# Graph network kernel: more of the gathered rows fetched by SyncE, at byte offsets loaded into registers

## The chip, the cores and the metric

The kernel runs on 1 core of one Trainium2 chip. The metric is the device time of one execution in microseconds. A chunk below is 8 steps, and a step is one edge of each of the 128 partitions.

## The reference

Three message-passing rounds over the same graph of 6250 nodes and 100000 edges, sorted by destination, with rows of 256 float32. Cut to what matters:

```python
def conv(x):                                   # round 0
    e = relu((x[dst] - x[src]) @ theta_w.T + theta_b + x[src] @ phi_w.T + phi_b)
    return where(isfinite(m := segment_max(e, dst)), m, 0.0)
def layers(x, he):                             # rounds 1 and 2
    hv = x @ W_in + b_in
    for W, b in ((W_u0, b_u0), (W_u1, b_u1)):
        m = relu(concatenate([hv[src], he]) @ W + b)
        hv = where(has_in, segment_max(m, dst) + hv, hv)
    return relu(hv @ W_ro + b_ro)
x = layernorm(x + conv(x)); x = layernorm(x + layers(x, edge_attr))
```

## The kernel before

The products with the weights are taken per node, not per edge. Each round r first writes a table in HBM (`table{r}`, 6272 rows of 256 float32, 1 KB each), then walks the edges in 782 steps. Partition p holds 782 consecutive edges of the sorted list, and step t handles edge t of every partition. So a step needs 128 rows of the table, chosen by `src`.

**GpSimd** fetches them, one indirect DMA per step, into the ring `gath` of G = 34 steps (`gather_edges`, L606). A pair of steps is handed over by one semaphore, and a slot is free again when PE has summed the group that read it (`group_summed`). In round 0 the first 34 steps read `x` itself and go through transposes and a product (`multiply_raw`).

**PE** moves each pair of rows into a bank of `edge_ps` by a product with the identity (L864 in round 0, L887 in rounds 1 and 2, where the product with the edge attributes at L885 comes first). It may be up to 3 (round 0) or 6 pairs ahead of DVE.

**DVE** keeps the running maximum along the edges, one `SCALAR_TENSOR_TENSOR` per step (L410), in the ring `hist` of H = 24 steps, three chunks. Before it writes the first state of a chunk it waits until the store of the chunk that had the same place has landed (`stored`). In round 0 it also searches, once per 16 steps, for the last edge of each node (L338, L341).

**SyncE** stores each chunk of states to `runs` in HBM (`store_runs`, L547), all of its work in one queue and one order. Ahead of the store of chunk c it calls `late_rows(r, c)`, and in round 0, for 49 of the chunks from chunk 20 on, it loads a piece of `x` (L542). The last three chunks are stored in pieces of two steps.

`late_rows` is what the change rewrites. For two groups of LATE = 4 steps in each round, beginning at steps 360 and 720, GpSimd issues nothing and SyncE fetches the rows one at a time, 4 x 128 = 512 for a group, in 32 batches of 16, one batch ahead of each of 32 chunks (chunks 11 to 42 and 56 to 87). A batch is a load of 16 row numbers from HBM into 16 registers (L526, `TENSOR_LOAD`), and then for each row a register operation (L529, `snap` and the product of row number and row length) and a DMA of 1 KB whose source offset is in a register (L530). The row numbers lie in `late_src`, which two DMAs at the start copy out of `src` (L562). The rows land in `late_sb`, and PE waits for the whole group at its first step (`wait_rows`).

After the steps of a round, partitions' ends are joined (L615, L618), the maxima of the nodes are gathered (L633), and the tables for the next round are made. The change does not touch that.

Of the kernel before, what the change touches and what calls it, by code (L numbers as in the profile page):

```python
# [5 lines left out]
P = 128  # L6
NODES, EDGES, D, ED = 6250, 100000, 256, 64
# [3 lines left out]
STEPS = 2 * -(-EDGES // (2 * P))  # L11
STRIDE = TURNS * BODY
# [5 lines left out]
SC = 8  # L18
# [9 lines left out]
NPAD = TILES * P  # L28

NU = -(-TILES // 2)  # L30
ROUNDS = 3
# [7 lines left out]
LATE_AT = (360, 720)  # L39
LATE = 4  # L40
LATE_ROWS = 16
# [3 lines left out]
FIRST_X_CHUNK = 20  # L45
assert TURNS == TILES and STRIDE % SC == 0 and H % SC == 0 and G % GS == 0 and STRIDE % HC == 0 and HC % GS == 0 and SC % GS == 0
# [3 lines left out]
def gnn_kernel(nc, a):  # L50
    f32, bf16, i32 = mybir.dt.float32, mybir.dt.bfloat16, mybir.dt.int32
# [8 lines left out]
    late_src = nc.dram_tensor("late_src", [len(LATE_AT), P * LATE], i32, kind="Internal").ap()  # L60
# [4 lines left out]
    with ctx:  # L65
        def sb(name, shape, dt=f32):
            return ctx.enter_context(nc.sbuf_tensor(name, shape, dt))

        def sem(name):
            return ctx.enter_context(nc.semaphore(name))  # L70
# [13 lines left out]
        late_sb = sb("late_sb", [P, LATE, D])  # L84
# [104 lines left out]
        late_landed = [sem(f"late_landed{n}") for n in range(ROUNDS * len(LATE_AT))]  # L189
# [30 lines left out]
        def groups_to(s):  # L220
            return s // STRIDE * GROUPS + min(s % STRIDE // GS + 1, GROUPS)

        def late_group(t):
            return next((n for n, first in enumerate(LATE_AT) if first <= t < first + LATE), None)

        def by_pool(t):
            return t < STEPS and late_group(t) is None
# [4 lines left out]
        def edge_rows(s):  # L232
            n = late_group(s % STRIDE)
            if n is not None:
                return late_sb[:, s % STRIDE - LATE_AT[n]:s % STRIDE - LATE_AT[n] + 2, :]
            return gath[:, s % G:s % G + 2, :]
# [5 lines left out]
        def all_written(sems, n):  # L242
            return [(sems[b], 16 * uses(n, b)) for b in range(UNIT_BUFS)]
# [19 lines left out]
        setup_at = {}  # L263
# [22 lines left out]
        def _(dve):  # L286
# [21 lines left out]
            dve.wait_ge(edges_loaded, 16 * len(edge_loads))  # L308
            dve.wait_ge(bits_loaded, 16 * len(edge_bits))
# [183 lines left out]
        def _(sp):  # L493
# [6 lines left out]
            def write_table(r, u):  # L500
                lo, hi = unit(u)
                sp.wait_ge(product_out, r * NU + u + 1)
                sp.dma_start(tables[r][lo * P:hi * P, :].rearrange("(k p) f -> p k f", p=P),
                             staged(u)).then_inc(staged_written[u % UNIT_BUFS], 16)
# [5 lines left out]

            late_regs = [nc.sync.alloc_register(f"late_reg{k}") for k in range(LATE_ROWS)]

            def late_rows(r, c):
                for n, first in enumerate(LATE_AT):
                    batches = P * LATE // LATE_ROWS
                    i = c - (first // SC - 2 - batches)
                    if not 0 <= i < batches:
                        continue
                    if i == 0 and n == 0:
                        sp.wait_ge(late_listed, 16 * len(LATE_AT))  # L520
                        for written, m in all_written(staged_written, r + 1):
                            sp.wait_ge(written, m)
                    if i == 0 and r + n > 0:
                        before = (r, n - 1) if n > 0 else (r - 1, len(LATE_AT) - 1)
                        sp.wait_ge(group_summed, groups_to(before[0] * STRIDE + LATE_AT[before[1]] + LATE - 1))
                    nc.sync.load(late_regs, late_src[n:n + 1, i * LATE_ROWS:(i + 1) * LATE_ROWS])  # L526
                    for k, reg in enumerate(late_regs):
                        p, t = divmod(i * LATE_ROWS + k, LATE)
                        row = nc.sync.snap(reg, min_val=0, max_val=NPAD - 1)  # L529
                        sp.dma_start(late_sb[p:p + 1, t, :], tables[r][bass.DynSlice(row, 1), :]  # L530
                                     ).then_inc(late_landed[r * len(LATE_AT) + n], 16)
# [28 lines left out]
            for n, first in enumerate(LATE_AT):  # L560
                with nc.allow_non_contiguous_dma("small layouts"):
                    sp.dma_start(late_src[n:n + 1, :].rearrange("o (p k) -> (o p) k", k=LATE), a["src"][:, first:first + LATE]  # L562
                                 ).then_inc(late_listed, 16)
            for u in range(NU):
                write_table(0, u)
            sp.wait_ge(setup_step, setup_at["none row"])
# [205 lines left out]
        def _(pe):  # L772
# [70 lines left out]
            def wait_rows(s):  # L843
                r, t = divmod(s, STRIDE)
                n = late_group(t)
                if n is None:
                    pe.wait_ge(gathered[s % G // 2], 2 * 16 * pairs_in_slot(s))
                elif t == LATE_AT[n]:
                    pe.wait_ge(late_landed[r * len(LATE_AT) + n], 16 * P * LATE)
# [128 lines left out]
```

## Time and profile before

| | |
|---|---|
| median of 3 runs | 4386.74 us (4368.79 to 4420.99) |
| span of the profiled execution | 3216.1 us |
| median less span | 1170.6 us |
| GpSimd busy | 2359.0 us, 73% |
| PE busy | 2494.2 us, 78% |
| DVE busy | 1457.3 us, 45% |
| DMA engines, mean busy | some 70%, 237 GB/s |

The profiled execution is recorded by its span alone, from the first to the last instruction; the time that the runs report holds 1170.6 us more. The three edge phases, from the first store of `runs` to the last state of a round, are where the time goes: about 925, 954 and 957 us. DMA issues, register loads and register operations of SyncE are not counted as busy, so its own load is read from the times at which its instructions start (marked SPq).

### The profile page before, as it was taken

Reading aid. Unit: us, or ns where it says so; the run is one execution under the profiler, and the core shown is the slowest. Engines: PE = TensorE matmul, PEld = TensorE weight load, DVE = VectorE, ACT = ScalarE, POOL = GpSimd, SP = SyncE. Lnnn points to the kernel's source line nnn. Section 1 sums busy time; section 2 is a strip of 40 time slices with the busy share of each in tenths; the row PEclk is TensorE's granted clock in tenths of the full one; section 3 lists DMA queues with packets and bytes.
Section 4 is the critical chain, followed back from the end, with each engine's and each line's share of the span. In section 5 each row is a group of like instructions: output and inputs, shape, how many; then the busy total and the mean of one; then the engine's idle time right before and its main releaser. Section 6 shows DMA issues by size and latency. Waiting matters only on the chain.

```text
span 3216.1 us, 33579 instructions
## 1 busy us (share of the span) xinstructions
PE 2494.2 (78%) x6386; PEld 1183.3 (37%) x6386; DVE 1457.3 (45%) x3424; ACT 196.1 (6%) x439; POOL 2359.0 (73%) x2484
## 2 busy tenths in 40 slices
PE   8776666666676888887887888688888888888877
PEld 6432222222223533333333333353333344333335
DVE  2675556555556533333433334323333343333337
ACT  2000000000002400000000000010000000000005
POOL 5777777777776677777777777667777777777765
PEclk9898888788877999999999999899999999999989
DMA  7666667666665777777777777687777777777764
GB/s 263 232 223 222 225 224 268 221 224 214 211 210 191 246 242 244 245 244 244 245 252 246 245 244 247 207 271 249 250 251 252 252 267 247 253 249 252 250 210 153
DMA packets 266593, 762.66 MB, mean 237 GB/s; under 512 B 57652, under 2 KB 113823, under 8 KB 229903
## 3 DMA queue, kind: packets, MB, share of 16 engines
q0 software_dynamic: 118896, 324.63, 33.2%
q1 hardware_dynamic: 94110, 356.95, 28.8%
q10 hardware_dynamic: 53376, 78.93, 7.9%
q14 instruction: 158, 1.29, 0.1%
q8 instruction: 53, 0.87, 0.1%
HBM read 413.88 MB, written 346.41 MB: 236 GB/s over the span
## 4 chain that ended last, share of the span: by engine, by line
POOL 39%; PE 17%; DMA 16%; issue 16%; SPq 7%; DVE 2%; ACT 2%; DVEq 0%; ACTq 0%; POOLq 0%
POOL gath L606 38%; DMA gath<-table,src_sb 14%; PE edge_ps L887 6%; SPq L530 4%; PE edge_ps L885 3%; PE edge_ps L778 3%; SPq L526 2%; PE side_ps L778 2%; PE edge_ps L864 2%; POOL gath L633 1%; DVE hist L410 1%; ACT x_sb L718 1%; DMA runs<-hist 1%; SPq L529 1%; DMA table<-hist 1%
## 5 line engine op out<-in xcount | busy, mean ns | idle before, releaser
L606 POOL DMA_INDIRECT gath<-table,src_sb x2288 | 2165.4, 946 | 745.0 <-issue 649.6
L410 DVE SCALAR_TENSOR_TENSOR hist<-hist,lift,edge_ps 128x256 f32<-128x256 f32 x2346 | 1127.0, 480 | 1564.3 <-PE edge_ps L887 1142.8
L887 PE MATMUL edge_ps<-gath,ident 128*128 128x512 f32 x1548 | 842.6, 627 | 328.0 <-DMA gath<-table,src_sb 326.4
L885 PE MATMUL edge_ps<-w_e,he_sb 128*128 128x512 f32 x1564 | 813.9, 602 | 5.5 <-DMA he_sb<-in_he 5.0
L864 PE MATMUL edge_ps<-gath,ident 128*128 128x512 f32 x740 | 476.3, 767 | 269.9 <-DMA gath<-table,src_sb 164.2
L887 PEld LDWEIGHTS edge_ps<-gath,ident 128*128 128x128 f32 x1548 | 275.7, 193 | 803.9 <-DMA gath<-table,src_sb 595.9
L885 PEld LDWEIGHTS edge_ps<-w_e,he_sb 128*128 128x128 f32 x1564 | 295.4, 194 | 352.7 <-issue 335.0
L864 PEld LDWEIGHTS edge_ps<-gath,ident 128*128 128x128 f32 x740 | 155.5, 236 | 532.5 <-DVE hist L410 317.1
L676 ACT COPY hv_sb<-side_ps 128x256 f32<-128x256 f32 x147 | 54.8, 373 | 2770.2 <-PE edge_ps L887 1842.9
L633 POOL DMA_INDIRECT gath<-runs,end_row x147 | 152.1, 1035 | 49.0 <-issue 43.6
L786 PE MATMUL edge_ps<-dst_f,onehot 128*128 128x512 f32 x200 | 78.0, 514 | 14.2 <-DVE onehot L333 14.2
L786 PEld LDWEIGHTS edge_ps<-dst_f,onehot 128*128 128x128 f32 x200 | 40.2, 205 | 71.2 <-issue 38.5
L778 PE MATMUL side_ps<-w_in_ro,back_T 128*128 128x256 f32 x196 | 60.1, 437 | 0.0
L778 PE MATMUL edge_ps<-w_ro,hist 128*128 128x256 f32 x196 | 50.4, 401 | 11.3 <-ACT hist L705 11.3
L778 PE MATMUL side_ps<-w_in_n,back_T 128*128 128x256 f32 x196 | 59.2, 431 | 0.0
L778 PE MATMUL edge_ps<-x_sb,hv_sb 128*128 128x256 f32 x196 | 45.7, 396 | 15.0 <-DVE x_sb L299 10.7
L778 PE MATMUL side_ps<-w_theta,hv_sb 128*128 128x256 f32 x196 | 55.4, 409 | 2.3 <-ACT hv_sb L676 2.3
L778 PE MATMUL side_ps<-w_ro,back_T 128*128 128x256 f32 x196 | 56.9, 418 | 0.0
L778 PEld LDWEIGHTS side_ps<-w_in_ro,back_T 128*128 128x128 f32 x196 | 43.0, 219 | 31.2 <-issue 27.2
L778 PEld LDWEIGHTS side_ps<-w_in_n,back_T 128*128 128x128 f32 x196 | 42.9, 219 | 31.3 <-issue 27.3
L341 DVE TENSOR_SCALAR_CACHE_REDUCE junk<-edge_ps,node_no 128x782 f32<-128x782 f32 x49 | 50.6, 1032 | 4.5
L778 PE MATMUL edge_ps<-w_in_n,hist 128*128 128x256 f32 x196 | 50.9, 390 | 0.0
(137 smaller groups left out, 1070.6 us busy)
## 6 DMA issues: line engine op xcount, KB each, us to landing
runs<-hist SPq DMA_DIRECT2D x285, 1024.0 KB, 5.0
he_sb<-in_he ACTq DMA_DIRECT2D x194, 256.0 KB, 2.9
late_sb<-table SPq DMA_DIRECT2D x3072, 1.0 KB
gath<-table,src_sb POOLq DMA_INDIRECT x2288, 3.4
table<-hist SPq DMA_DIRECT2D x72, 256.0 KB, 3.4
back_T<-x1T ACTq DMA_DIRECT2D x98, 128.0 KB, 3.2
runs<-hist SPq DMA_DIRECT2D x33, 256.0 KB, 2.9
x_sb<-in_x SPq DMA_DIRECT2D x49, 128.0 KB, 2.8
```

The costliest lines, as they stand in the source:

```text
L341: V.tensor_scalar(junk[:, :], query_ps[:, 0:STEPS], nodes, 0.0, ALU.is_lt, ALU.add, accum_out=counts[:, 1:2])
L410: state = V.scalar_tensor_tensor(hist[:, s % H, :], hist[:, (s - 1) % H, :], lift[:, t:t + 1], edges, ALU.add, ALU.max)
L526: nc.sync.load(late_regs, late_src[n:n + 1, i * LATE_ROWS:(i + 1) * LATE_ROWS])
L530: sp.dma_start(late_sb[p:p + 1, t, :], tables[r][bass.DynSlice(row, 1), :]).then_inc(late_landed[r * len(LATE_AT) + n], 16)
L606: pool.indirect_dma_start(gath[:, s % G, :], None, a["x"] if s < RAW else tables[r], bass.IndirectOffsetOnAxis(src_sb[:, t:t + 1], 0)).the ...
L633: pool.indirect_dma_start(rows(u)[:, k, :], None, runs[0:SPARE, :], bass.IndirectOffsetOnAxis(end_row[:, lo + k:lo + k + 1], 0)).then_inc( ...
L676: A.copy(hv_sb[:, n % TILES, :], back_ps).then_inc(back_kept, 1)
L778: last = T.matmul(to, left, right, start=(m == 0), stop=(bias is None and m == len(terms) - 1))
L786: last = T.matmul(query_ps[:, lo:hi], onehot[:, :], dst_f[:, lo:hi], start=True, stop=True)
L864: last = T.matmul(edge_bank(0, t), ident[:, :], flat(edge_rows(t)), start=True, stop=True)
L885: T.matmul(bank, he_sb[:, c % NHE, at:at + P], w_e[r - 1][:, :], start=True, stop=False)
L887: last = T.matmul(bank, ident[:, :], flat(edge_rows(s)), start=False, stop=True)
```

## The change

SyncE fetches 14 steps of each round instead of 8, as seven pairs that begin at steps 120, 222, ..., 732. It does 20 rows ahead of every store instead of 16 ahead of some, from chunk 0 on, until the 7 x 256 rows of the round are issued (chunk 89). The rows of a chunk come in two batches, 16 and 4 as a rule. GpSimd skips these 14 steps. DVE multiplies the 14 columns of `src` by 1024 on chip at the start, SyncE writes the products to `late_list` behind its table write 12, and the DMA's source is a flat byte view of the table, so that a loaded register is the offset itself. Each load has registers of its own. `late_sb` becomes two buffers of one pair.

```diff
-LATE_AT = (360, 720)
-LATE = 4
-LATE_ROWS = 16
+LATE = 2
+LATE_PAIRS = 7
+LATE_EVERY, LATE_FIRST = 102, 120
+LATE_BUFS = 2
+LATE_PER_CHUNK = 20
+LATE_LOAD = 16
+ROW_BYTES = 4 * D
+LIST_UNIT = 12
...
-        late_sb = sb("late_sb", [P, LATE, D])
+        late_sb = sb("late_sb", [P, LATE_BUFS, LATE, D])
+        late_at = sb("late_at", [P, LATE_PAIRS, LATE], i32)
...
+            for n in range(LATE_PAIRS):
+                last = V.tensor_scalar(late_at[:, n, :], src_sb[:, late_step(n):late_step(n) + LATE], ROW_BYTES, None,
+                                       ALU.mult)
+            reached("late offsets", last)
...
             def late_rows(r, c):
-                for n, first in enumerate(LATE_AT):
-                    batches = P * LATE // LATE_ROWS
-                    i = c - (first // SC - 2 - batches)
-                    if not 0 <= i < batches:
-                        continue
...
-                    nc.sync.load(late_regs, late_src[n:n + 1, i * LATE_ROWS:(i + 1) * LATE_ROWS])
-                    for k, reg in enumerate(late_regs):
-                        p, t = divmod(i * LATE_ROWS + k, LATE)
-                        row = nc.sync.snap(reg, min_val=0, max_val=NPAD - 1)
-                        sp.dma_start(late_sb[p:p + 1, t, :], tables[r][bass.DynSlice(row, 1), :]
-                                     ).then_inc(late_landed[r * len(LATE_AT) + n], 16)
+                total = LATE_PAIRS * P * LATE
+                i, end = min(c * LATE_PER_CHUNK, total), min((c + 1) * LATE_PER_CHUNK, total)
+                while i < end:
+                    n, at = divmod(i, P * LATE)
+                    m = r * LATE_PAIRS + n
+                    count = min(LATE_LOAD, end - i, P * LATE - at)
...
+                    if at == 0 and m >= LATE_BUFS:
+                        was_r, was_n = divmod(m - LATE_BUFS, LATE_PAIRS)
+                        sp.wait_ge(group_summed, groups_to(was_r * STRIDE + late_step(was_n)))
+                    regs = [nc.sync.alloc_register(f"late{r}_{i + k}") for k in range(count)]
+                    nc.sync.load(regs, late_list[n:n + 1, at:at + count])
+                    for k, reg in enumerate(regs):
+                        p, t = divmod(at + k, LATE)
+                        offset = nc.sync.snap(reg, donate=True, min_val=0, max_val=(NPAD - 1) * ROW_BYTES)
+                        sp.dma_start(late_sb[p:p + 1, m % LATE_BUFS, t, :].bitcast(mybir.dt.uint8),
+                                     table_bytes[r][bass.DynSlice(offset, ROW_BYTES)].rearrange("(o f) -> o f", o=1)
+                                     ).then_inc(late_landed[m], 16)
+                    i += count
...
             for u in range(NU):
                 write_table(0, u)
+                if u == LIST_UNIT:
+                    sp.wait_ge(setup_step, setup_at["late offsets"])
+                    with nc.allow_non_contiguous_dma("small layouts"):
+                        sp.dma_start(late_list.rearrange("n (p k) -> p n k", k=LATE), late_at[:, :, :]
+                                     ).then_inc(late_listed, 16)
```

On SyncE, in a chunk with late rows before (the ISA is the register operation; L547 is the store of the states to `runs`):

```order
L547 DMA runs<-hist 128x2048
L526 TENSOR_LOAD late_src
L529 ISA
L530 DMA late_sb<-table 1x256
L529 ISA
```

The last two rows alternate 16 times up to the next store. In the changed kernel the same chunk reads so (L565 is the store now):

```order
L565 DMA runs<-hist 128x2048
L542 TENSOR_LOAD late_list
L546 DMA late_sb<-table 1x1024 x16
L542 TENSOR_LOAD late_list
L546 DMA late_sb<-table 1x1024 x4
L565 DMA runs<-hist 128x2048
```

The register operations are gone, four rows and a second load have come, and 1024 bytes stand for 256 float32. A move of a register is not shown in such rows.

On SyncE at the start of round 0, between the loads and the first states, before:

```order
L562 DMA late_src<-in_src 128x4 x2
L503 DMA table<-hist 128x2x256 x24
L503 DMA table<-hist 128x256
L567 DMA runs<-x_sb 1x256
L547 DMA runs<-hist 128x2048 x11
```

And in the changed kernel:

```order
L519 DMA table<-hist 128x2x256 x13
L583 DMA late_list<-late_at 128x7x2
L519 DMA table<-hist 128x2x256 x11
L519 DMA table<-hist 128x256
L586 DMA runs<-x_sb 1x256
L542 TENSOR_LOAD late_list
L546 DMA late_sb<-table 1x1024 x16
```

The list is written in the middle of the table writes, and the eleven stores that had no late rows ahead of them now have 20 each.

On GpSimd, the gathers of rounds 0 and 1, before:

```order
L606 DMA gath<-in_x,src_sb 128x256 x34
L606 DMA gath<-table,src_sb 128x256 x740
L615 DMA fix_rows<-runs,fix_from 128x256
L618 DMA runs<-fix_rows,fix_to 100225x256
L633 DMA gath<-runs,end_row 128x256 x49
L606 DMA gath<-table,src_sb 128x256 x774
```

And in the changed kernel:

```order
L625 DMA gath<-in_x,src_sb 128x256 x34
L625 DMA gath<-table,src_sb 128x256 x734
L634 DMA fix_rows<-runs,fix_from 128x256
L637 DMA runs<-fix_rows,fix_to 100225x256
L652 DMA gath<-runs,end_row 128x256 x49
L625 DMA gath<-table,src_sb 128x256 x768
```

Six gathers fewer stand in each of the three rounds.

## Rows read from the trace of the kernel before

**Rows 1.** The page's first line, and its chain by engine (shares of the span)

```profile
span 3216.1 us, 33579 instructions
...
POOL 39%; PE 17%; DMA 16%; issue 16%; SPq 7%; DVE 2%; ACT 2%; DVEq 0%; ACTq 0%; POOLq 0%
```

**Rows 2.** Groups of GpSimd, 1093.3 to 2061 us: busy us, mean ns | idle, releasers

```profile
L606 POOL DMA_INDIRECT gath<-table,src_sb x774 | 731.6, 945 | 253.1 <-issue 218.5 <-DMA table<-hist 17.6 <-PE edge_ps L887 17.1
```

**Rows 3.** Chain of waits, 300 to 330 us, by line

```profile
by line: SPq L530 41.0%; SPq L526 22.9%; issue 21.9%; SPq L529 6.8%; SPq L547 4.3%; SPq L542 3.7%
```

**Rows 4.** Timeline of SyncE, round 0 with x_sb loads: start us, us, what

```profile
275.59 0.42 SPq L547 DMA_DIRECT2D runs<-hist  x1
...
315.31 0.37 SPq L542 DMA_DIRECT2D x_sb<-in_x  x1
315.73 0.43 SPq L547 DMA_DIRECT2D runs<-hist  x1
...
476.02 0.42 SPq L547 DMA_DIRECT2D runs<-hist  x1
```

**Rows 5.** Timeline of SyncE, stores without x_sb loads, rounds 0 and 2

```profile
180.85 0.37 SPq L547 DMA_DIRECT2D runs<-hist  x1
...
255.42 0.36 SPq L547 DMA_DIRECT2D runs<-hist  x1
...
2862.10 0.36 SPq L547 DMA_DIRECT2D runs<-hist  x1
...
2928.21 0.35 SPq L547 DMA_DIRECT2D runs<-hist  x1
```

**Rows 6.** Waits of SyncE's queue, 1220 to 1520 and 1540 to 1660 us: us, times, longest

```profile
SPq L547 <- DVE hist L410: 12.5, 14, 2.4
...
SPq L547 <- DVE hist L410: 116.2, 13, 12.6
```

**Rows 7.** Groups of DVE, 400 to 450 us

```profile
L410 DVE SCALAR_TENSOR_TENSOR hist<-hist,lift,edge_ps 128x256 f32<-128x256 f32 x40 | 19.2, 480 | 22.4 <-DMA runs<-hist 19.1 <-issue 0.4
```

**Rows 8.** Lines L526, L529, L530: duration ns min/median/max, first and last start

```profile
L526 SPq TENSOR_LOAD <-late_src x192: 1855/2114/2909, 171.6 to 3019.6; - x192
...
L529 SPq FUSED_REGOPS  x3072: 44/44/59, 173.5 to 3028.3; - x192
...
L530 SPq MOVE late_sb<-table x3072: 29/29/38, 173.6 to 3028.4; - x192
L530 SPq DMA_DIRECT2D late_sb<-table x3072: 224/228/929, 173.7 to 3028.4; - x192
```

**Rows 9.** Timeline of PE, round 1, with the rows at hand

```profile
1541.07 1.02 PE L885 MATMUL edge_ps<-w_e,he_sb 128*128 128x512 f32 x2
1541.92 1.02 PE L887 MATMUL edge_ps<-gath,ident 128*128 128x512 f32 x2
```

**Rows 10.** Timeline of SyncE, the first store of each round

```profile
74.13 0.36 SPq L547 DMA_DIRECT2D runs<-hist  x1
...
1110.95 0.33 SPq L547 DMA_DIRECT2D runs<-hist  x1
...
2162.54 0.33 SPq L547 DMA_DIRECT2D runs<-hist  x1
```

**Rows 11.** Timeline of DVE, the last two states of each round

```profile
998.08 1.04 DVE L410 SCALAR_TENSOR_TENSOR hist<-hist,lift,edge_ps 128x256 f32<-128x256 f32 x2 [1.32 <-PE edge_ps L864]
...
2063.91 1.04 DVE L410 SCALAR_TENSOR_TENSOR hist<-hist,lift,edge_ps 128x256 f32<-128x256 f32 x2 [0.68 <-PE edge_ps L887]
...
3118.24 1.04 DVE L410 SCALAR_TENSOR_TENSOR hist<-hist,lift,edge_ps 128x256 f32<-128x256 f32 x2 [0.68 <-PE edge_ps L887]
```

**Rows 12.** Line L562, the list of late rows at the start

```profile
L562 SPq DMA_DIRECT2D late_src<-in_src x2: 611/922/1232, 3.2 to 3.8; - x2
...
DMA to landing us min/median/max: 15.4/17.2/18.9
```

**Rows 13.** Line L410, idle time of DVE before it: us, times

```profile
  DMA runs<-hist: 88.4, 24
```

More of the change, by code:

```diff
@@ L59, in gnn_kernel @@
     msgT = nc.dram_tensor("msgT", [P, TILES * D], f32, kind="Internal").ap()
-    late_src = nc.dram_tensor("late_src", [len(LATE_AT), P * LATE], i32, kind="Internal").ap()
+    late_list = nc.dram_tensor("late_list", [LATE_PAIRS, P * LATE], i32, kind="Internal").ap()
+    table_bytes = [t.rearrange("n f -> (n f)").bitcast(mybir.dt.uint8) for t in tables]
     halves = lambda w: w.rearrange("(h k) o -> k h o", h=KH)
@@ L188, in gnn_kernel @@
         late_listed = sem("late_listed")
-        late_landed = [sem(f"late_landed{n}") for n in range(ROUNDS * len(LATE_AT))]
+        late_landed = [sem(f"late_landed{n}") for n in range(ROUNDS * LATE_PAIRS)]
         fix_turned = sem("fix_turned")
@@ L221, in groups_to, with late_step, late_pair @@
             return s // STRIDE * GROUPS + min(s % STRIDE // GS + 1, GROUPS)
-        def late_group(t):
-            return next((n for n, first in enumerate(LATE_AT) if first <= t < first + LATE), None)
+        def late_step(n):
+            return LATE_FIRST + n * LATE_EVERY
+        def late_pair(t):
+            n, k = divmod(t - LATE_FIRST, LATE_EVERY)
+            return n if 0 <= n < LATE_PAIRS and k < LATE else None
         def by_pool(t):
-            return t < STEPS and late_group(t) is None
+            return t < STEPS and late_pair(t) is None
         def pairs_in_slot(s):
@@ L232, in edge_rows @@
         def edge_rows(s):
-            n = late_group(s % STRIDE)
+            r, t = divmod(s, STRIDE)
+            n = late_pair(t)
             if n is not None:
-                return late_sb[:, s % STRIDE - LATE_AT[n]:s % STRIDE - LATE_AT[n] + 2, :]
+                return late_sb[:, (r * LATE_PAIRS + n) % LATE_BUFS, :, :]
             return gath[:, s % G:s % G + 2, :]
@@ L509, in write_turned @@
                 sp.dma_start((x1T, msgT)[r][:, lo * D:hi * D], flat(turned(u))).then_inc(turned_written[u % UNIT_BUFS], 16)
-            late_regs = [nc.sync.alloc_register(f"late_reg{k}") for k in range(LATE_ROWS)]
             def late_rows(r, c):
-                for n, first in enumerate(LATE_AT):
-                    batches = P * LATE // LATE_ROWS
-                    i = c - (first // SC - 2 - batches)
-                    if not 0 <= i < batches:
-                        continue
[L519 to L525, printed above, removed]
-                    nc.sync.load(late_regs, late_src[n:n + 1, i * LATE_ROWS:(i + 1) * LATE_ROWS])
-                    for k, reg in enumerate(late_regs):
-                        p, t = divmod(i * LATE_ROWS + k, LATE)
-                        row = nc.sync.snap(reg, min_val=0, max_val=NPAD - 1)
-                        sp.dma_start(late_sb[p:p + 1, t, :], tables[r][bass.DynSlice(row, 1), :]
-                                     ).then_inc(late_landed[r * len(LATE_AT) + n], 16)
@@ new lines, in late_rows @@
+                total = LATE_PAIRS * P * LATE
[4 more added lines that the diff above has]
+                    count = min(LATE_LOAD, end - i, P * LATE - at)
+                    if i == 0:
+                        for written, k in all_written(staged_written, r + 1):
+                            sp.wait_ge(written, k)
+                        sp.wait_ge(late_listed, 16)
+                    if at == 0 and m >= LATE_BUFS:
[10 more added lines that the diff above has]
+                    i += count
@@ L558, in write_out @@
                     sp.dma_start(a["out"][lo * P:NODES, :], outs(u)[0:left, 0, :]).then_inc(out_written[u % UNIT_BUFS], 16)
[L560 to L563, printed above, removed]
             for u in range(NU):
                 write_table(0, u)
+                if u == LIST_UNIT:
[3 more added lines that the diff above has]
+                                     ).then_inc(late_listed, 16)
             sp.wait_ge(setup_step, setup_at["none row"])
@@ L844, in wait_rows @@
                 r, t = divmod(s, STRIDE)
-                n = late_group(t)
+                n = late_pair(t)
                 if n is None:
                     pe.wait_ge(gathered[s % G // 2], 2 * 16 * pairs_in_slot(s))
-                elif t == LATE_AT[n]:
-                    pe.wait_ge(late_landed[r * len(LATE_AT) + n], 16 * P * LATE)
+                else:
+                    pe.wait_ge(late_landed[r * LATE_PAIRS + n], 16 * P * LATE)
             def first_rows():
```

## The prediction

> **What bounds the kernel now.** I read the page's first line and its chain of waits. The span is 3216.1 us, and GpSimd is the largest share of the chain at 39%, with SyncE's queue (SPq) at 7% [rows 1]. The share of GpSimd's busy time is not the point; its regularity is. In round 1 its 774 table gathers stand with 731.6 us busy, 218.5 us of plain issue and 17.1 us put down to PE [rows 2]. That is 967.2 / 774 = 1.25 us from one gather to the next, and the 17.6 us behind table<-hist belong to the start of the round. So GpSimd never really waits inside a round: it issues at its own pace and sets the length of rounds 1 and 2. A chunk of 8 steps costs it 8 x 1.25 = 10.0 us.
>
> Next comes the engine to which the work is given. In the stretch from 300 to 330 us the chain runs through SyncE alone: its row DMAs 41.0%, its register loads 22.9%, its register operations 6.8% [rows 3]. The page as a whole hides this. Twenty stores of round 0, each with an x_sb load and 16 late rows ahead of it, stand between 275.59 and 476.02 us: 10.02 us each [rows 4]. Without the x_sb load it is (255.42 - 180.85) / 8 = 9.32 us in round 0, and (2928.21 - 2862.10) / 7 = 9.44 us in round 2 [rows 5]. In these stretches the store follows the last row at once. In round 1, between 1220 and 1520 us, some 30 stores wait only 12.5 us for DVE in sum, while in 120 us without late rows they wait 116.2 us [rows 6]. So where late rows are fetched SyncE has at most half a microsecond of slack per chunk, and in round 0 its slow stores already stall the states: 19.1 us of 50 between 400 and 450 us, waiting for runs<-hist [rows 7]. GpSimd does not feel it there because the rings (34 steps of gath, 24 of hist) absorb it and there is time to recover in chunks without late rows.
>
> **What the change removes.** GpSimd drops from 774 to 768 gathers of table rows a round (740 to 734 in round 0): 18 x 1.25 = 22.5 us, if GpSimd remains the limit. SyncE loses the fused register operation (44 ns, and about 36 ns until the next instruction starts: 80 ns) per row. The MOVE in rows 8 stands on the DMA's own line, L530, not on the line of snap, so I take it to stay: a DMA with an offset in a register needs it. The bytes per row stay 1024.
>
> **What it adds.** From 2 x 32 batches of 16 rows a round to 1792 rows, 20 in each of 90 of the 98 chunks, and two register loads per chunk (16 and 4 registers) where there was one. Stretches without late rows, in which SyncE recovered, are gone but for the last 8 chunks.
>
> Per chunk, from the measured 16-row chunk (row spacing inside a batch: 44 + 29 + 228 ns and some 120 ns between the three, 0.42 us [rows 8]):
> - minus 16 x 0.08 = -1.28 us (register operation gone);
> - plus 4 rows x 0.34 (29 + 228 ns and two gaps) = +1.36 us;
> - plus the gaps around a second load = +0.11 us;
> - plus the second load itself, L. The trace has loads of 16 registers only: 1855 / 2114 / 2909 ns [rows 8].
>
> L is the unknown. From above it is the same 2.11 us, if the time is one trip to memory; from below it is 4/16 of it, 0.53 us, if it goes by registers. The other sequencer instructions beside it are small (29 to 44 ns), so I expect most of a load to go with its count of registers, with some fixed part: 0.5 fixed and 0.1 per register fits the 16, and gives L = 0.9 us for four. I keep both ends.
>
> The Trainium skill, "DMA: Bandwidth & Descriptors", section "Latency and other measured facts", gives a floor of about 600 ns for such a load; no run here shows it. With that floor and the rest linear, four registers would be an estimated 0.98 us, some 20 us more over the program than by my 0.9. The skill's "Runtime: NRT & Kernel Launch", section "Instruction fetch mechanics", speaks of about 200 ns per register, which would make 3.2 us of sixteen; the trace's 2.11 disagrees.
>
> The sum per chunk is T = T16 + 0.19 + L: with L = 0.9, 9.4 + 1.1 = 10.5 us in round 0, 10.0 + 1.1 = 11.1 with an x_sb load, and 9.5 + 1.1 = 10.6 in rounds 1 and 2 (9.44 and a little for the stalls of single row DMAs, up to 929 ns in rows 8). GpSimd needs 768 / 782 x 10.0 = 9.8 us per chunk. SyncE is now the slowest engine of every chunk with late rows, and in order: each store of runs stands behind 20 rows, the ring of hist holds three chunks, so DVE waits for stores, PE for banks, GpSimd for free slots of gath. The edge phase then lasts from the first store through 89 more chunks of SyncE, and a tail. In the tail everything but PE and DVE is ahead: late pair 6 stands at step 732, and its last rows are issued ahead of store 89, so about 50 steps are left. A pair of steps costs PE two groups of 0.86 us in rounds 1 and 2 [rows 9], so 25 x 1.72 + 3 us for the side products = 46 us. In round 0 DVE sets it: of the 50 us of [rows 7] it waited 19.1 for stores, so 40 states with their share of the searches took 30.9, 0.77 us a step, and 50 steps some 40 us.
>
> - Round 0: before, first store 74.1 [rows 10], last state ends at 999.1 [rows 11]. After: the store comes at about 76 (10 us of rows behind the last table write). 76 + 49 x 11.1 + 40 x 10.5 + 40 = 1080: +81 us.
> - Round 1: first store 1110.95 (DVE sets it, SyncE has its 10 us free there), 89 x 10.6 = 943, +46: 2100 against 2065: +35 us.
> - Round 2: 2162.5 + 943 + 46 = 3152 against 3119: +33 us.
> - The list: one DMA of 896 pieces of 8 bytes behind table write 12, where two of 128 pieces stood at the start (0.61 and 1.23 us of issue, 17.2 us to land [rows 12]). Landing lies beside 12 more table writes; I charge 3 us, bounds 0 and 8. The seven small DVE operations lie in front of a wait for dst. The data moved is the same (2304 rows of 1 KB from one queue to the other), so I charge nothing to the DMA engines.
>
> The joins, the gathers of maxima and the table products are not touched. Sum: 81 + 35 + 33 + 3 = 152 us. The span goes to about 3368. The time outside the span, 4386.7 - 3216.1 = 1170.6 us by the median (the profiled execution has only its span), I keep, so 4386.7 + 152 = 4539 us, 3.5% slower. Per microsecond of L the three rounds change by 267 us: at 0.53 us it is -99, so +53 (4440); at 2.11 us +323, so +475 (4862).
>
> **Rivals.**
> - *SyncE stays hidden and GpSimd's six gathers per round are won.* The trace leaves 9.8 us per chunk for SyncE. If the MOVE went with the fused operation (0.06 us x 20 = 1.2 us) or a row cost under 0.28 us, T would be 10.6 - 1.2 = 9.4 us in rounds 1 and 2 and 9.9 with an x_sb load. Below 9.8 us, GpSimd decides, and all that is left is 18 x 1.25 = 22.5 us: 4364 us, not slower. For it: the operands of each row come ready from a load. Against it: the MOVE's line, and the DMA's own 224 to 228 ns, which alone with one gap makes 0.27 us.
> - *The second load costs as much as the first.* Then T is 11.8 us, and the kernel comes to 4862 us. For it: the loads of 16 vary from 1.86 to 2.91 us, as trips to a busy memory do. Against it: nothing that ties the time to the count either; the two are told apart only by a load of another size.
> - *SyncE is the limit by a hair.* L near 0.53 and no further stalls: 4440 us; the low end of my forecast, not a case of its own.
> - *Rows land too late for PE.* PE would wait for late_sb before SyncE's stores are the limit. Pair n is used at step 120 + 102 n, chunk 15 + 12.75 n, and is issued by chunk 12.8 (n + 1): 1.9 to 2.2 chunks ahead, some 20 us. It would only show once SyncE lags anyway, and add a few us.
>
> **How the numbers follow.** Forecast (SyncE limits, L between 0.5 and 1.5): 0.62, its own range 4440 to 4700. Second load at full price: 0.13. SyncE hidden: 0.20, 4364. Something that I don't see, split on both sides: 0.05. The range for 8 in 10 takes in the hidden case at its lower end and leaves out most of the full price: 4364 to 4720. A measurement of this kernel tells about 1% from no change, that is 44 us, and its three runs before lie 52 us apart. The most that the change can win is half of that, so faster by over 1% gets 0.03; within 1% the hidden case and the lowest edge of the forecast, 0.24; slower 0.73.
>
> **What would show it.** Right: stores of runs 10.5 to 11.1 us apart with no wait for DVE in nearly all chunks up to 89, DVE's idle time behind runs<-hist grown from 88 us [rows 13] to several hundred, GpSimd gathers spaced over 1.3 us late in each round, and row DMAs 0.34 us apart; round 0 grows most. Wrong: loads of four registers at 2.1 us (too low a forecast), row spacing under 0.29 us, or gathers still at 1.25 us throughout (hidden). If round 0 grows and rounds 1 and 2 shrink, T lies near 9.8 us and L near zero.

## The result, and the profile after

The changed kernel took 4573.12 us (median of 4 runs, 4523.43 to 4612.19) beside 4393.26 us for the kernel before on the same chip: ratio 1.0346, 95% interval 1.0268 to 1.0424, so slower by 3.5%. The ratio leaves out the slow run of 4612.19 us; the two medians, with it, lie 180 us or 4.1% apart.

One thing has to be said before any line is read. This kernel runs at two levels of time, and every series of runs, each on one chip, was at one of them throughout. No chip is known to have had two series, so whether the chip or the hour decides is not told apart. In the series above and in two later ones the kernel before took 4393, 4336 and 4369 us; in the four others it took 3218 to 3224 us. The trace of before that stands ahead of the prediction (span 3216.1 us) is of the lower level, the runs beside it of the upper one, and no trace of the kernel before at the upper level is on record. The time outside the span is about 2 us in every run that has both (4523.43 us is a span of 4521.6), not 1170. At the lower level the changed kernel took 3275.18 us beside 3219.19: ratio 1.0177 (1.0159 to 1.0196), 56 us slower. So the change loses at both levels: 56 us at the lower, 154 and 180 us at the upper.

The first trace of after is of the upper level. The page's first line, its chain by engine and line, and the states' group in part 5:

```profile
span 4521.6 us, 35449 instructions
...
SPq 59%; issue 29%; PE 6%; another core or an unknown queue 2%; DVE 1%; ACT 1%; DMA 1%; POOL 0%; DVEq 0%; ACTq 0%; POOLq 0%
SPq L546 41%; SPq L542 16%; PE edge_ps L797 2%; SPq L565 2%; PE edge_ps L906 1%; PE edge_ps L904 1%; DVE hist L426 0%; SPq L560 0%; ACT x_sb L737 0%; PE edge_ps L883 0%; PE edge_ps L917 0%; PE side_ps L917 0%; DMA runs<-hist 0%; ACT hist L676 0%
...
L426 DVE SCALAR_TENSOR_TENSOR hist<-hist,lift,edge_ps 128x256 f32<-128x256 f32 x2346 | 1125.6, 480 | 2790.8 <-DMA runs<-hist 2208.0
```

GpSimd held 39% of the chain in [rows 1] and now holds nothing; SyncE's queue has 59%, nearly all of it in the rows (L546) and the register loads (L542). DVE's wait for stores was 88.4 us in [rows 13] and is 2208.

The line of the row DMAs and the line of the stores in the same trace (duration ns min/median/max, first and last start; the last row tells who waited for the stores, us and times):

```profile
L546 SPq MOVE late_sb<-table x5376: 1/29/1414, 88.1 to 4351.3; - x200
L546 SPq DMA_DIRECT2D late_sb<-table x5376: 1/228/1423, 88.2 to 4351.3; - x200
...
L565 SPq DMA_DIRECT2D runs<-hist x318: 2/355/1305, 98.5 to 4404.9; - x159
...
  DVE hist L426: 2227.0, 251
```

The medians are those of [rows 8], but a MOVE of 29 ns takes up to 1.4 us here. The chain of waits from 1999 to 2014 us shows how (start us, us, what):

```profile
1999.61 0.72 SPq L546
2000.33 0.02 issue
2000.34 0.70 SPq L546
2001.04 0.71 issue
2001.75 0.69 SPq L546
2002.44 0.70 issue
2003.14 0.70 SPq L546
```

Step after step costs 0.7 us here, instruction or pause. Ten microseconds later a whole chunk runs at full speed, 20 rows in 7.74 us, from store to store 10.2 us:

```profile
2013.81 0.33 SPq L565 DMA_DIRECT2D runs<-hist  x1
2016.27 7.74 SPq L546 DMA_DIRECT2D late_sb<-table  x20
2024.06 0.35 SPq L565 DMA_DIRECT2D runs<-hist  x1
```

Over the 4839 spacings of neighbouring rows the median is 0.32 us. Those over 0.4 us hold 1284 us more than that in this trace, and 53 us in the changed kernel's trace at the lower level. That is about the 1248 us by which the two spans differ. Of SyncE's 11831 records 1197 last 650 to 750 ns (123 at the lower level), and 1016 last under 10 ns (2 at the lower level, where even a MOVE has 29). So in places the times of the records may themselves be late.

Most of the other work is as fast: a gather takes 947 ns (947 in the changed kernel at the lower level), a state 480 ns (480), and a packet of the gathers' queue 0.239 x 4521.6 x 16 / 118032 = 146 ns, with 144 in the first trace of before. The packets that fetch instructions took 130 us in sum at either level, so SyncE did not wait for slower ones. TensorE alone differs: its mean granted clock was 0.786 against 0.891, and its products took longer. First a line of the upper level, then the same of the lower:

```profile
L904 PE MATMUL edge_ps<-w_e,he_sb 128*128 128x512 f32 x1564 | 938.9, 686 | 752.3 <-DVE hist L426 443.9
```

```profile
L904 PE MATMUL edge_ps<-w_e,he_sb 128*128 128x512 f32 x1564 | 845.8, 624 | 65.1 <-DVE hist L426 59.3
```

PE was busy for 2715 us against 2535, which is at most 180 of the 1248 us, and it stood idle far more (busy 60% of the span against 77%). No run tells whether its lower clock is a cause or follows from that.

### The profile page after: what moved, and what is told of

Read it like the earlier page. It is cut to its first block, busy times and chain, and to the rows that moved or that the text cites. A ratio compares the mean times of both kernels' runs of the same rounds, so it can differ in the third digit from the quotient of the medians.

```text
span 4521.6 us, 35449 instructions
## 1 busy us (share of the span) xinstructions
PE 2715.0 (60%) x6386; PEld 1308.5 (29%) x6386; DVE 1455.7 (32%) x3431; ACT 195.4 (4%) x439; POOL 2333.5 (52%) x2466
## 3 DMA queue, kind: packets, MB, share of 16 engines
q0 software_dynamic: 118032, 322.27, 23.9%
## 4 chain that ended last, share of the span: by engine, by line
SPq 59%; issue 29%; PE 6%; another core or an unknown queue 2%; DVE 1%; ACT 1%; DMA 1%; POOL 0%; DVEq 0%; ACTq 0%; POOLq 0%
SPq L546 41%; SPq L542 16%; PE edge_ps L797 2%; SPq L565 2%; PE edge_ps L906 1%; PE edge_ps L904 1%; DVE hist L426 0%; SPq L560 0%; ACT x_sb L737 0%; PE edge_ps L883 0%; PE edge_ps L917 0%; PE side_ps L917 0%; DMA runs<-hist 0%; ACT hist L676 0%
## 5 line engine op out<-in xcount | busy, mean ns | idle before, releaser
L426 DVE SCALAR_TENSOR_TENSOR hist<-hist,lift,edge_ps 128x256 f32<-128x256 f32 x2346 | 1125.6, 480 | 2790.8 <-DMA runs<-hist 2208.0
L904 PE MATMUL edge_ps<-w_e,he_sb 128*128 128x512 f32 x1564 | 938.9, 686 | 752.3 <-DVE hist L426 443.9
L906 PE MATMUL edge_ps<-gath,ident 128*128 128x512 f32 x1536 | 872.5, 652 | 10.5 <-DMA gath<-table,src_sb 10.5
L883 PE MATMUL edge_ps<-gath,ident 128*128 128x512 f32 x734 | 516.9, 851 | 523.2 <-DVE hist L426 319.0
L904 PEld LDWEIGHTS edge_ps<-w_e,he_sb 128*128 128x128 f32 x1564 | 317.1, 217 | 1185.8 <-issue 658.9
L906 PEld LDWEIGHTS edge_ps<-gath,ident 128*128 128x128 f32 x1536 | 326.9, 213 | 452.4 <-issue 436.3
L883 PEld LDWEIGHTS edge_ps<-gath,ident 128*128 128x128 f32 x734 | 186.1, 270 | 793.9 <-DVE hist L426 411.2
L652 POOL DMA_INDIRECT gath<-runs,end_row x147 | 142.5, 970 | 81.6 <-issue 43.0
L906 PE MATMUL edge_ps<-late_sb,ident 128*128 128x512 f32 x28 | 29.1, 1141 | 172.3 <-DMA late_sb<-table 172.3
L797 PE MATMUL edge_ps<-w_n,hist 128*128 128x256 f32 x196 | 52.8, 418 | 18.7 <-issue 10.0
```

Source lines behind the costliest of these rows:

```text
L426: state = V.scalar_tensor_tensor(hist[:, s % H, :], hist[:, (s - 1) % H, :], lift[:, t:t + 1], edges, ALU.add, ALU.max)
L652: pool.indirect_dma_start(rows(u)[:, k, :], None, runs[0:SPARE, :], bass.IndirectOffsetOnAxis(end_row[:, lo + k:lo + k + 1], 0)).then_inc( ...
L797: last = T.matmul(to, left, right, start=(m == 0), stop=(bias is None and m == len(terms) - 1))
L883: last = T.matmul(edge_bank(0, t), ident[:, :], flat(edge_rows(t)), start=True, stop=True)
L904: T.matmul(bank, he_sb[:, c % NHE, at:at + P], w_e[r - 1][:, :], start=True, stop=False)
L906: last = T.matmul(bank, ident[:, :], flat(edge_rows(s)), start=False, stop=True)
```

## The experiments

**The kernel before, unchanged.**

> The kernel before, unchanged, to see whether its 3216 us span is what it usually does. Theory A (slow stretches: in the changed kernel's trace SyncE's instructions stand in stretches of some 0.7 us each, 1290 us in sum over the plain row spacing of 0.32 us; the kernel before has them too in most executions, and its one trace was taken in an execution without them): span within 5 us of the time, near 4390 us, and row spacings over 0.52 us by the hundred. Theory B (1170 us lie outside the span in the kernel before and vanish in the changed one): span 3216 us again with a time of 4390.

Measured: 3218.9 us (10 runs, 3215.81 to 3220.54), span 3217.6; beside it the reference runs of the kernel before had a median of 3218.73 (25 runs). Neither theory's number: span and time agree to 2 us, but at 3219, not at 4390. So no 1170 us lie outside the span, and the levels belong to a whole series, not to single executions. Theory B falls.

**One load per chunk.**

```diff
-LATE_LOAD = 16
+LATE_LOAD = 20
```

> The changed kernel with all 20 registers of a chunk in one load (two only where a pair ends). Theory A (SyncE's queue sets the time; a second load is 0.6 to 0.7 us): 89 x 3 x 0.3 us saved at the least, 60 to 200 us under the changed kernel. Rival (the loads are not what costs, the slow stretches follow the number of rows): within 1% of the changed kernel.

Measured: 3218.3 us beside 3218.73, ratio 1.000 (0.999 to 1.001). The expectation compared with the changed kernel, whose time at this level came later: 3275.2. The difference is 57 us, just below the 60 to 200 expected. The load of 20 registers has a median of 2.60 us, where the two loads had 2.10 and 0.76. So without the second load nothing is left of the loss at the lower level. The three rounds took 948.3, 956.5 and 958.0 us, where the kernel before had 934.3, 961.8 and 965.6 (trace below): the gathers saved in rounds 1 and 2 just pay for what SyncE still costs in round 0.

**Eight steps, fetched in the new way.**

```diff
-LATE_PAIRS = 7
-LATE_EVERY, LATE_FIRST = 102, 120
+LATE_PAIRS = 4
+LATE_EVERY, LATE_FIRST = 186, 204
-LATE_PER_CHUNK = 20
+LATE_PER_CHUNK = 11
```

> The changed kernel's way of fetching, but for 8 steps of each round as before (4 pairs, 11 rows ahead of each store, one load each). Theory A (cost per instruction of SyncE): a chunk has 24 instructions of SyncE instead of 43, 5.5 us plain and some 8 with slow stretches, under GpSimd's 9.8: span 3200 to 3400 us. Rival (the cost comes with any row DMA at a byte offset, or lies elsewhere than in SyncE's queue): near the changed kernel, 4300 us or more.

Measured: 3218.8 us, ratio 1.0002 (0.9992 to 1.0011): as the theory said, and the same as the kernel before. The byte offsets, with no more rows than before, bring nothing, since SyncE is hidden either way. A surprise stands in its loads (L542, ns min/median/max):

```profile
L542 SPq TENSOR_LOAD <-late_list x291: 640/5154/6717, 63.9 to 3077.6; - x146
```

A load of 11 registers takes 5.2 us where one of 16 takes 2.1. SyncE's chunk was 9 us for 11 rows, not 5.5; see the last section.

**The same row DMAs at fixed offsets.**

```diff
-                    regs = [nc.sync.alloc_register(f"late{r}_{i + k}") for k in range(count)]
-                    nc.sync.load(regs, late_list[n:n + 1, at:at + count])
-                    for k, reg in enumerate(regs):
+                    for k in range(count):
...
-                        offset = nc.sync.snap(reg, donate=True, min_val=0, max_val=(NPAD - 1) * ROW_BYTES)
+                        offset = (p * TILES + t) * ROW_BYTES
...
-                                     table_bytes[r][bass.DynSlice(offset, ROW_BYTES)].rearrange("(o f) -> o f", o=1)
+                                     table_bytes[r][offset:offset + ROW_BYTES].rearrange("(o f) -> o f", o=1)
```

This kernel leaves out the choice of rows by `src`: the late steps get fixed rows of the table, and its output is another one. The bytes moved are the same.

> The changed kernel with the same 5376 row DMAs at offsets known when the program is built: no register loads and no moves (the late steps get fixed rows of the table). Theory A (cost per instruction of SyncE, loads dear): 21 instructions a chunk, 5.8 us plain, about 8 with slow stretches: span 3200 to 3400 us. Rival (the DMAs of 1 KB themselves block the queue, as all go to one ring): 4300 us or more, slow stretches as long as in the changed kernel.

Measured: 3194.4 us, ratio 0.9930 (0.9913 to 0.9946): 24.3 us faster than before, where 18 gathers fewer are 22.5 us. So what the change wanted to win is there to be won as soon as SyncE needs less than GpSimd. Its chunk was 8 us, not 5.8: the DMAs follow each other at 0.29 us, and nearly every chunk has one or two that take about a microsecond (L544):

```profile
L544 SPq DMA_DIRECT2D late_sb<-table x5376: 214/253/1654, 63.9 to 3022.8; - x200
```

**The changed kernel again.**

> The changed kernel, unchanged, beside the kernel before on one chip, since the kernel before took 3219 us in 25 executions of the last series and 4393 us in the four of the first. Theory A (the slow stretches of 0.7 us per instruction belong to the chip or session of the first measurement; without them SyncE needs 0.4 + 2.1 + 0.65 + 20 x 0.32 + 0.3 = 9.9 us a chunk, 10.5 with an x_sb load, GpSimd 9.8): span 3225 to 3270 us, 0 to 1.5% slower than before, most of it in round 0; if before is again at 4390, the changed kernel at 4520 to 4620. Theory C (the slow stretches come with the changed kernel's own instructions: registers of its own, two loads): near 4550 us even where before takes 3219.

Measured: 4490.35 us (4463.66 to 4509.40) beside 4336.11 (4313.86 to 4346.71), ratio 1.0374 (1.0329 to 1.0419). The upper level again, and a loss of 154 us. The trace repeats the first: the row spacings over 0.4 us hold 1235 us more than the median. The number for the upper level (4520 to 4620) was missed by 30 us.

**Before and after at the lower level.** Of three kernels in one series, the first was the kernel before, the second the changed one.

> The kernel before once more, for its trace on a chip of this series. The chips differ: on one it takes 3219 us, on another 4336 us. Theory A (on a slow chip SyncE's instructions take some 0.7 us each while the gathers move, and nothing of it on a fast chip): where the time is over 4300 us, over 1000 us of SyncE's row spacings stand above the plain 0.42 us, and stores with late rows come 15 to 18 us apart, stores without them 10 us apart as ever; where it is 3219 us, as in the first trace. Rival (on a slow chip everything is slower: transfers, gathers, clock): stores without late rows come over 12 us apart as well.

Measured: 3217.8 us, lower level; it said nothing about the upper.

> The changed kernel, unchanged. On a fast chip by theory A: 3225 to 3270 us beside 3219 (SyncE needs about 10 us a chunk, GpSimd 9.8). On a slow chip 4450 to 4620 us beside 4310 to 4420, as in the first series. Theory C (slow stretches come with the changed kernel): over 4400 us on a fast chip too.

Measured: 3275.18 us (3273.33 to 3281.04) beside 3219.19, ratio 1.0177. A few us above the expected range, and far from 4400: theory C falls. This is the trace that can be held against the prediction's working, since both sides are of one level. Rows, stores and loads (L546, L565, L542), and then two chunks of round 1 on SyncE's timeline:

```profile
L546 SPq MOVE late_sb<-table x5376: 29/29/29, 64.4 to 3123.3; - x200
L546 SPq DMA_DIRECT2D late_sb<-table x5376: 227/228/1385, 64.5 to 3123.4; - x200
...
L565 SPq DMA_DIRECT2D runs<-hist x318: 319/355/654, 73.7 to 3177.5; - x159
...
L542 SPq TENSOR_LOAD <-late_list x537: 636/1497/3830, 62.4 to 3117.9; - x179
```

```profile
1501.18 0.35 SPq L565 DMA_DIRECT2D runs<-hist  x1
1503.54 7.23 SPq L546 DMA_DIRECT2D late_sb<-table  x20
1510.82 0.35 SPq L565 DMA_DIRECT2D runs<-hist  x1
1513.57 7.79 SPq L546 DMA_DIRECT2D late_sb<-table  x20
1521.41 0.36 SPq L565 DMA_DIRECT2D runs<-hist  x1
```

9.6 and 10.6 us from store to store, with 20 rows and two loads in each, and the store issues right behind the last row. The 7.23 us hold the second load too (20 rows alone are 6.4). The states by round, first and last start (L426, one row for each round):

```profile
L426 DVE SCALAR_TENSOR_TENSOR hist<-hist,lift,edge_ps x782: 479/480/482, 66.6 to 1043.6; 128x256 f32<-128x256 f32 x196
...
L426 DVE SCALAR_TENSOR_TENSOR hist<-hist,lift,edge_ps x782: 479/480/483, 1147.3 to 2109.9; 128x256 f32<-128x256 f32 x196
...
L426 DVE SCALAR_TENSOR_TENSOR hist<-hist,lift,edge_ps x782: 479/480/483, 2198.6 to 3177.0; 128x256 f32<-128x256 f32 x196
```

Lengths 977.0, 962.6 and 978.4 us. The same view of the kernel before, from a later series at the lower level:

```profile
L410 DVE SCALAR_TENSOR_TENSOR hist<-hist,lift,edge_ps x782: 479/480/482, 67.3 to 1001.6; 128x256 f32<-128x256 f32 x196
...
L410 DVE SCALAR_TENSOR_TENSOR hist<-hist,lift,edge_ps x782: 479/480/484, 1105.4 to 2067.2; 128x256 f32<-128x256 f32 x196
...
L410 DVE SCALAR_TENSOR_TENSOR hist<-hist,lift,edge_ps x782: 479/480/483, 2156.1 to 3121.7; 128x256 f32<-128x256 f32 x196
```

These are 934.3, 961.8 and 965.6 us. What the changed kernel's states (DVE) and then its gathers (GpSimd) waited for at the lower level (idle us, times):

```profile
  DMA runs<-hist: 794.4, 174
```

```profile
  PE edge_ps L883: 59.1, 79
  PE edge_ps L906: 36.9, 121
```

DVE's wait for stores rose from 88 to 794 us, while GpSimd was hardly held up: in rounds 1 and 2 its gathers still came 1.25 us apart, all 768 of them.

**No late rows at all.** The third kernel of that series.

```diff
-LATE_AT = (360, 720)
+LATE_AT = ()
```

> The kernel before without any late rows: GpSimd gathers all 782 steps, SyncE only stores. Theory A (row DMAs on SyncE's queue are what makes a slow chip slow): 24 gathers more, 30 us, so about 3249 us on a fast chip and between 3240 and 3300 us on a slow one as well, over 1000 us under both kernels there. Rival (the slow chip is slow in itself): 4300 us or more there.

Measured: 3246.72 us, ratio 1.0088 (1.0071 to 1.0105), 3249 expected: 24 gathers of 1.25 us are 30, and 27.5 are seen. It fell on the lower level, so the part on the upper one stayed open. A further series had this kernel and the kernel before:

> The kernel without late rows again, for a slow chip (before at 4310 to 4420 us); on fast ones it took 3247 us. Theory A (SyncE's row instructions are what is slow there): 3240 to 3300 us on a slow chip. Rival (the slow chip is slow in itself): 4300 us or more.

> The kernel before again, for its trace on a slow chip. Theory A: span near 4330 to 4400 us, over 1000 us of SyncE's row spacings above the plain 0.42 us, stores with late rows 15 to 18 us apart, stores without them 10 us as ever. On a fast chip: 3216 to 3224 us.

Measured: 3247.8 and 3220.85 us, the lower level once more. Both say nothing on the upper.

**A different way in each round.** One kernel puts both questions to one trace. Its core, set in the kernel before (the list of offsets is made as in the change):

```diff
+                    if r == 0:
+                        continue
...
-                    nc.sync.load(late_regs, late_src[n:n + 1, i * LATE_ROWS:(i + 1) * LATE_ROWS])
+                    nc.sync.load(late_regs, (late_src if r == 1 else late_list)[n:n + 1, i * LATE_ROWS:(i + 1) * LATE_ROWS])
...
+                        if r == 1:
+                            row = nc.sync.snap(reg, min_val=0, max_val=NPAD - 1)
...
+                        offset = nc.sync.snap(reg, donate=True, min_val=0, max_val=(NPAD - 1) * 4 * D)
```

> The kernel before with its late rows changed round by round: none in round 0 (GpSimd gathers all), as before in round 1, and in round 2 the same 64 batches of 16 rows but at byte offsets, with no register operation. Theory A (on a slow chip it is SyncE's row instructions that take 0.7 us each while gathers move, so a chunk with late rows costs about the sum of both engines' times): on a slow chip the edge phase of round 0 lasts 930 to 960 us as on a fast one, that of round 1 some 390 us longer than its 962, that of round 2 some 250 us longer (33 instructions a chunk instead of 50). Rival (a slow chip is slow in itself): all three rounds longer alike. On a fast chip: 3228 us in all (8 gathers more in round 0), and SyncE's chunk 1.3 us shorter in round 2 than in round 1 without any gain in time, as GpSimd paces both.

Measured: 4048.5 us (4031.4 and 4065.61) beside 4368.78, ratio 0.926 (0.913 to 0.939): the upper level. The states by round:

```profile
L416 DVE SCALAR_TENSOR_TENSOR hist<-hist,lift,edge_ps x782: 479/480/483, 91.2 to 1197.4; 128x256 f32<-128x256 f32 x196
...
L416 DVE SCALAR_TENSOR_TENSOR hist<-hist,lift,edge_ps x782: 479/480/483, 1319.5 to 2619.4; 128x256 f32<-128x256 f32 x196
...
L416 DVE SCALAR_TENSOR_TENSOR hist<-hist,lift,edge_ps x782: 479/480/482, 2724.6 to 3913.0; 128x256 f32<-128x256 f32 x196
```

Round 1, as before: 1299.9 us, 338 over the 961.8 of the lower level (390 expected). Round 2, the same rows with no register operation: 1188.4, 223 over 965.6 (250 expected). But round 0, with no late rows at all, took 1106.2 us, where the kernel without late rows took 939.5 for it at the lower level (68.5 to 1008.0). Theory A had said 930 to 960, so it fails there, and the rival is true for its part: some 167 us of the round at the upper level have nothing to do with late rows. If the other two rounds hold as much of it, late rows cost 171 us in the old way and 56 at byte offsets.

The byte offsets, worth nothing at the lower level, are thus worth 115 us a round here. That is little more than the plain price of what they leave out, 1024 register operations of 0.10 us with their gap (rows 0.42 us apart become 0.32), 99 us. So this run shows that SyncE is no longer hidden at the upper level, and not that each of its instructions costs more there.

In that round the profile puts DVE's waits down so (us, times, longest):

```profile
DVE hist L416 <- remote: 275.3, 68, 11.1
DVE hist L416 <- PE edge_ps L881: 150.5, 62, 11.5
DVE hist L416 <- issue: 50.2, 39, 8.9
```

"remote" is a semaphore update whose writer the trace does not hold. The traces of the upper level lack most records of landings (22363 stand in the changed kernel's, 64320 in its trace at the lower level): the page's issue rows (part 6) give a time to landing at the lower level, and none at the upper. First the changed kernel's row at the lower level, then at the upper:

```profile
runs<-hist SPq DMA_DIRECT2D x285, 1024.0 KB, 4.7
```

```profile
runs<-hist SPq DMA_DIRECT2D x285, 1024.0 KB
```

So at the upper level the path on which semaphore updates and instruction records travel looks congested, and SyncE's stretches of 0.7 us per step may be the same thing. That is argued, not shown: no run here changes that path alone. The runs of the later series all have a span beside their time, so they were themselves recorded, and how long the kernel takes at that level without a recording is not known.

**Six pairs, 16 rows a chunk.**

```diff
-LATE_PAIRS = 7
-LATE_EVERY, LATE_FIRST = 102, 120
+LATE_PAIRS = 6
+LATE_EVERY, LATE_FIRST = 126, 146
-LATE_PER_CHUNK = 20
+LATE_PER_CHUNK = 16
```

> The changed kernel with 6 pairs of steps in place of 7 and 16 rows ahead of each store in place of 20, so one load of 16 registers a chunk. Theory A (the changed kernel loses on a fast chip because its chunk of SyncE, 10.3 us, is longer than GpSimd's 9.8): here SyncE needs 0.4 + 2.1 + 16 x 0.32 + 0.4 = 8.0 us, 8.7 with an x_sb load, GpSimd sets the time again and its 12 gathers fewer than before are won: 15 us, 3204 us beside 3219 on a fast chip. On a slow chip 33 instructions of SyncE in 96 chunks stand against 50 in 64: 4100 to 4300 us beside 4310 to 4420. Rival (spreading the rows over all chunks is what costs, whatever their number): 3240 us or more on a fast chip.

Measured: 3214.56 us (11 runs, 3211.38 to 3219.80) beside 3223.92 (15 runs), ratio 0.9972 (0.9963 to 0.9981): 9 us faster than the kernel before, of 15 expected, and 2% faster than the changed kernel by the two ratios. The queue has slack again (who SyncE's stores waited for: us, times, longest), where the changed kernel at the lower level had 157.5 us in 58 times:

```profile
SPq L565 <- DVE hist L426: 506.3, 230, 11.2
```

The rival falls: the spread over all chunks costs at most the 6 us that are missing. The gathers came 1.253 us apart here instead of 1.250, 7 us over the program, which fits the 5 us by which the kernel before is up. Where the 6 us went stays open, and the upper level was not measured.

## Why the prediction was right or wrong

The forecast was 4539 us, 3.5% slower, by one mechanism: SyncE's chunk becomes longer than GpSimd's. Measured were 4573 us and 3.5%. The direction holds at both levels. The mechanism is shown at the lower one, where taking out the second load or four rows a chunk takes the loss away. At the upper one it is argued, and there alone the size agrees: 180 and 154 us against 152. That agreement is luck, and the steps must be taken apart.

**The step on the time outside the span failed.** "The time outside the span, 4386.7 - 3216.1 = 1170.6 us [...] I keep" took a difference between two levels for a fixed cost of a run. The span and the time belong to different levels, and a gap of a quarter of the time should have been called a doubt about the trace, not a term of the sum. The 152 us were worked out on rows of the lower level, where the measured loss is 56.

**Held against the trace of the same level, the terms stand so.**
- A row 0.34 us: measured 0.32. The MOVE stayed, as argued from its line, and the register operation had taken 0.10 us with its gap, not 0.08.
- L = 0.9 us for four registers: measured 0.76. Grouping the 537 loads by the rows that follow them gives medians of 0.76, 1.17, 1.60 and 2.10 us for 4, 8, 12 and 16, so 0.31 us fixed and 0.11 per register, close to the 0.5 and 0.1 assumed.
- T of 10.5, 11.1 and 10.6 us: from the first store to the ninetieth a chunk took 10.37, 10.17 and 10.30 us in the three rounds, where the forecast had 10.83 (the mean of 10.5 and 11.1 by their counts), 10.6 and 10.6. L accounts for 0.14 us of that and the rows for up to 0.35, less some for single slow DMAs. Over 3 x 89 chunks this mis-sized term is 106 us too much.
- The tails of 40 and 46 us: from the ninetieth store to the end of the last state 47 in round 0, 51 in round 1 and 54 in round 2, together 20 us more than forecast. The two make up most of the way from 152 to 57; the rest is small (3 us for the list, 2 us at the first store).
- The rounds: +81, +35, +33 predicted; 977.0 - 934.3 = +43, +1 and +13 measured. The order is right, with round 0 as the worst because of its x_sb loads. In round 1 GpSimd and SyncE came out even: as much as the 7.5 us of six gathers was given back.
- The sensitivity, 267 us per microsecond of L, told that the answer hangs on a load of four registers; the kernel with one load confirms it. At the lower end of L the working gave +53 us, and +56 was seen, but L was not at that end: with the measured 0.76 the working gives +115, and the cheaper rows bring the rest.

**Of the rivals:** "SyncE stays hidden" did not come about, but its price was right. With fixed offsets 24 us were won where 22.5 were worked out. The full price of the second load is refuted (0.76 us, not 2.1). "Rows land too late for PE" was called a few us more once SyncE lags. PE waited for late rows 66 us in 8 times in rounds 1 and 2 and 32 us in 5 times in round 0 at the lower level, where it waited 3.5 us once before: larger than was said. It fits the same lag of SyncE, seen at another place, and the kernel with one load has none of it in rounds 1 and 2.

**What the prediction would have shown wrong** was partly seen: GpSimd's gathers stayed at 1.25 us in rounds 1 and 2 at the lower level. The buffers (34 steps of gath, 24 of hist) took the whole lag of SyncE, 0.35 to 0.5 us a chunk, until the late rows ended. The test named there was too strict: an engine can set the end of a round without ever stopping the one that paced it before.

**Why the change costs 154 to 180 us at the upper level** is argued only. The one round with late rows in the old way that has a trace there took 1300 us, in another series, and the changed kernel's three took 1347.5, 1378.5 and 1359.1: 48 to 79 us more each. It fits that SyncE has more instructions in all (43 instead of 50 a chunk, but in 90 chunks instead of 64), which can meet the same 0.7 us stretches. Without a trace of the kernel before at that level this cannot be split, and why the stretches come at all stays open.

## What to carry to other kernels

Before work goes from a pacing engine to a queue with slack, add up the queue's plain time per period, with each register load at its own price, and keep the total under the pacing engine's: here 10.3 us against 9.8 lost 56 us, and about 8 won 9. Make the register load one per period, and let its start and its count be multiples of 4 words, as those of the quick loads here were. When span and measured time disagree by more than some microseconds, find out which of the two the runs reproduce before any duration of the trace is used.

## What the hardware showed that was not expected

- The same program takes 3218 to 3224 us in some series and 4336 to 4393 us in others, steadily within a series (25 runs from 3215 to 3224; 7 runs from 4314 to 4347). Gathers, states and packets are as fast in both; SyncE's instructions stand in stretches of 0.7 us each, TensorE's mean granted clock is lower (0.80 against 0.92 for the kernel before), and most landings leave no record.
- A register load of 16 words took 2.1 us and one of 4 words 0.76, but one of 11 words 5.2 us. The place in memory makes most of it. Loads of 11 words that begin at a multiple of 4 words of the list took 2.55 us (median of 72, 2.23 to 3.54), those that begin elsewhere 5.3 (198 loads, 4.77 to 6.72). The count has its part: 11 words from such a place took 2.55 us where 12 took 1.60. The three loads of 1 word in that kernel took 0.64 to 0.70.
- DMAs of 1 KB at fixed offsets, 0.29 us apart with nothing between them, ran into single ones of up to 1.65 us in nearly every chunk, so that leaving out loads and moves brought 20 rows only from 9.6 to about 7.5 us.
